# LN1's shift in per-sequence biases, h's low part on VectorE, both normal forms on GpSimd

## The reference, cut to what matters

```python
mod = (_silu(L0_c) @ L0_wmod).reshape(L0_c.shape[0], 6, 1, -1)
sa, ca, ga, sb, cb, gb = (mod[:, 0], mod[:, 1], mod[:, 2], mod[:, 3], mod[:, 4], mod[:, 5])
ga = (2 * (ga >= 0) - 1) * jnp.maximum(jnp.abs(ga), 0.25)      # gb alike
h = _layernorm(x, axis=-1) * (1 + ca) + sa
x = x + ga * attention(h)        # q, k, v = h @ w.T + bias; softmax over |i-j| <= 32; @ wo.T + bo
h = _layernorm(x, axis=-1) * (1 + cb) + sb
x = x + gb * ffn(h)              # top 2 of 8 gated SiLU experts, and the shared one
```

## Time and profile before

| what | value |
|---|---|
| median of 3 runs | 743.09 us (741.37 to 744.73) |
| the profiled execution | 748.45 us |
| its span, first to last instruction | 746.7 us |
| TensorE (PE) busy | 661.9 us, 89% |
| ScalarE (ACT) busy | 590.7 us, 79% |
| VectorE (DVE) busy | 581.9 us, 78% |
| GpSimd (POOL) busy | 567.4 us, 76% |
| DMA, mean over the span | 171 GB/s |
| mean granted TensorE clock | 0.924 |

### The profile page before, as it was taken

How to read it: one execution, slowest core, us unless ns; L and a number is a source line. 1 busy time by engine, 2 the same in 40 slices (tenths; PEclk the granted TensorE clock), 3 DMA queues, 4 the chain that set the end, 5 groups by cost and what they waited for, 6 DMA issues and landing times.

```text
span 746.7 us, 18990 instructions
## 1 busy us (share of the span) xinstructions
PE 661.9 (89%) x5934; PEld 556.9 (75%) x5934; DVE 581.9 (78%) x1541; ACT 590.7 (79%) x2538; POOL 567.4 (76%) x628
## 2 busy tenths in 40 slices
PE   2278898999999999989998999989899989989886
PEld 1167676878878788878887888878788878878775
DVE  5446656988888888979898689888898978867553
ACT  3277777989898989889898689889898988875442
POOL 5440518998989888996988599988979896758784
PEclk9655557999999999999999899999999999999999
DMA  4747675777785867767777668677777676614120
GB/s 146 181 104 181 176 203 138 186 214 191 199 210 170 214 186 202 192 186 205 187 180 192 175 187 206 185 187 209 196 193 207 160 211 158 197 33 137 54 90 14
DMA packets 193860, 127.70 MB, mean 171 GB/s; under 512 B 110640, under 2 KB 170848, under 8 KB 193632
## 3 DMA queue, kind: packets, MB, share of 16 engines
q1 hardware_dynamic: 193760, 126.50, 64.0%
HBM read 96.29 MB, written 30.17 MB: 169 GB/s over the span
## 4 chain that ended last, share of the span: by engine, by line
PE 47%; DMA 17%; SPq 10%; POOL 9%; issue 7%; ACT 6%; DVE 4%; POOLq 0%; DVEq 0%; ACTq 0%
DMA k<-k_scr 11%; PE ps_s L1218 11%; PE ps_Y L1286 10%; SPq L315 6%; PE ps_O L1241 6%; DMA r_scr<-rst 5%; ACT p L686 4%; PE ps_A L1160 3%; POOL xl L503 3%; POOL xs L497 2%; SPq L323 2%; PE ps_A L1162 2%; PE ps_A L1161 2%; PE ps_M L1269 2%; PE ps_B L1160 2%
## 5 line engine op out<-in xcount | busy, mean ns | idle before, releaser
L686 ACT ACTIVATE p<-ps_s,nmx 128x96 f32<-128x96 f32 x1024 | 332.7, 347 | 52.7 <-DVE nmx L886 52.4
L686 ACT ACTIVATION_READ_ACCUMULATOR p<-ps_s,nmx 128x1 f32 x1024 | 218.2, 213 | 0.0
L1218 PE MATMUL ps_s<-k,q 128*128 128x96 f32 x1024 | 168.8, 299 | 54.0 <-DMA k<-k_scr 35.3
L1218 PEld LDWEIGHTS ps_s<-k,q 128*128 128x128 f32 x1024 | 147.6, 211 | 84.5 <-DMA k<-k_scr 42.4
L886 DVE TENSOR_REDUCE nmx<-ps_s 128x4 f32<-128x384 f32 x256 | 137.9, 547 | 59.9 <-PE ps_s L1218 56.2
L503 POOL TENSOR_TENSOR xl<-xs,xh 128x512 fp32r<-128x512 f32 x128 | 162.9, 1278 | 21.1 <-ACT xh L708 21.1
L497 POOL TENSOR_TENSOR xs<-h,sbc 128x512 f32<-128x512 f32 x128 | 163.6, 1284 | 1.8 <-DMA sbc<-s_scr 1.7
L1286 PE MATMUL ps_Y<-w2s,g 128*128 128x128 f32 x1152 | 161.4, 288 | 0.6 <-DVE g L992 0.6
L1286 PEld LDWEIGHTS ps_Y<-w2s,g 128*128 128x128 f32 x1152 | 148.5, 200 | 4.7 <-DVE g L992 0.8
L903 DVE STREAM_TRANSPOSE pt<-p 128x384 f32<-128x384 f32 x256 | 136.6, 558 | 17.3 <-ACT p L686 14.5
L983 DVE SCALAR_TENSOR_TENSOR th<-th,ps_A 128x512 f32<-128x512 f32 x144 | 97.6, 678 | 33.4 <-ACT th L729 32.1
(11 more groups left out here) (119 smaller groups left out, 931.2 us busy)
## 6 DMA issues: line engine op xcount, KB each, us to landing
sbc<-s_scr SPq DMA_DIRECT2D x64, 512.0 KB, 5.6
k<-k_scr SPq DMA_DIRECT2D x64, 384.0 KB
q<-q_scr SPq DMA_DIRECT2D x128, 96.0 KB
k<-k_scr SPq DMA_DIRECT2D x32, 336.0 KB
q_scr<-qh SPq DMA_DIRECT2D x32, 256.0 KB, 2.8
k_scr<-kh SPq DMA_DIRECT2D x32, 256.0 KB, 3.0
xt<-x SPq DMA_DIRECT2D x16, 256.0 KB, 6.1
q_scr<-ql SPq DMA_DIRECT2D x16, 256.0 KB, 2.9
```

The source lines that it names most:

```text
L686: last = nc.scalar.activation(p[:, n % PRING, gg, :], ps_s[:, n % 2, MK * gg:MK * gg + MK], ACT.Exp, bias=nmx[:, n, gg:gg + 1], accum_out= ...
L1218: last = mm(ps_s[:, n % 2, MK * gg:MK * gg + MK], heads[:, h, gg, nl], k4[:, h, gg, :, MB * nl:MB * nl + MB], start=gg == 0, stop=gg == HG ...
```

## The change

- LN1's shift sa is no longer added to h. The projections see h = xn x (1 + ca), and W sa + bias is made once for each sequence at the start, in `bqk` for q and k and `bvs` for v: three matmuls of 16 columns, three VectorE operations, a fourth slice in wqkv (wv in its own order). The matmul through wo now takes `bvs`, one bias for each sequence.
- `modulate` of LN1 and the tile h1 go. `high_h1` makes hh from the PSUM bank M1, with the scale.
- `low_h1` moves from GpSimd to VectorE: hl = scale x M1 - hh from PSUM. Its call stands behind `moments(b-1, l2)` and ahead of `low_q(b+1)`.
- `normal` of LN2 moves from ScalarE (behind `probabilities(b, 8)`) to GpSimd (behind `shift(b-1, l2)`, ahead of `expand_v(b, 0)`).
- SyncE: `put_q`, `put_k`, `load_half`, `spread_scores` and `spread_sums` are cut into smaller calls, called in the same order of DMAs, with further waits (shown). `load_bias` waits for `add_bias` of the sequence before.

```diff
@@ SyncE @@
             def load_bias(b):
+                if b > 0:
+                    sp.wait_ge(xb_d, b)
                 sp.dma_start(brow[:], b_scr[bass.ds(b, 1)].to_broadcast([128, D])).then_inc(b_in, 16)
...
+            def put_ql(b, par):
+
                 sp.wait_ge(q_l, b + 1)
+                if b >= 2:
+                    sp.wait_ge(half_in[0], 112 * (b - 1))
+                    sp.wait_ge(half_in[1], 112 * (b - 1))
                 sp.dma_start(q_scr[par, :, 1].rearrange("j r s -> r j s"), ql[:].bitcast(F32)).then_inc(q_scr_w, 16)
...
+            def put_scores(b):
 
                 sp.wait_ge(smt_cp, b + 1)
+                if b > 0:
+                    for k in range(NE // 2):
+                        sp.wait_ge(s_in[k], 16 * b)
                 sp.dma_start(s_scr, smT[:]).then_inc(s_wr, 16)
...
+            def put_sums(b):
 
                 sp.wait_ge(rst_cp, b + 1)
+                if b > 0:
+                    sp.wait_ge(r_in, 16 * b)
@@ GpSimd @@
-            def low_h1(b):
-
-                pool.wait_ge(l1["hh"], b + 1)
-                nc.gpsimd.tensor_tensor(hl[:], h1[:], hh[:].bitcast(F32), ALU.subtract).then_inc(l1["hl"], 1)
...
                 if has(b, 2):
                     scaled_low(b - 2, 3, par)
-                if has(b, -1, 1):
-                    low_h1(b + 1)
-                if has(b, 2):
                     scaled(b - 2, 4, par)
                 if has(b, 1):
                     spread_var(b - 1, l2, ln2)
                     inverse(b - 1, l2, ln2)
                     shift(b - 1, l2, ln2)
+                    normal(b - 1, l2, ln2, x2[:, 1 - par])
                 if has(b, 0, 1):
                     expand_v(b, 0)
@@ ScalarE @@
-            def normal(b, s, ln, src):
...
             def high_h1(b):
 
-                act.wait_ge(l1["h"], b + 1)
-                if not seq_is(b, 0):
+                act.wait_ge(l1["tr"], b + 1)
+                if b == 0:
+                    act.wait_ge(s_md, 1)
+                else:
                     act.wait_ge(v_mm, b)
                     act.wait_ge(q_mm, b)
-                nc.scalar.activation(hh[:], h1[:], ACT.Copy).then_inc(l1["hh"], 1)
+                nc.scalar.activation(hh[:], ps["M1"][:], ACT.Copy, scale=col(mod, 1, b)).then_inc(l1["hh"], 1)
...
-                nc.scalar.activation(qh[:], ps["M1"][:], ACT.Identity, bias=bqs[:]).then_inc(q_h, 1)
+                nc.scalar.activation(qh[:], ps["M1"][:], ACT.Identity, bias=col(bqk, 0, b)).then_inc(q_h, 1)
...
                 if has(b, -1, 1):
-                    modulate(b + 1, l1, h1[:], 0, "M1")
                     high_h1(b + 1)
...
                 if has(b, 0):
                     probabilities(b, 8, par)
-                if has(b, 1):
-                    normal(b - 1, l2, ln2, x2[:, 1 - par])
-                if has(b, 0):
                     probabilities(b, 9, par)
@@ VectorE @@
+            def low_h1(b):
+
+                dve.wait_ge(l1["hh"], b + 1)
+                nc.vector.scalar_tensor_tensor(hl[:], ps["M1"][:], col(mod, 1, b), hh[:].bitcast(F32),
+                                               ALU.mult, ALU.subtract).then_inc(l1["hl"], 1)
...
+            dve.wait_ge(s_sa, 1)
+            nc.vector.tensor_scalar(bqk[:, 0], ps["M0"][:, 0:B], bia[:, 0:1], SCALE, ALU.add, ALU.mult)
+            nc.vector.tensor_scalar(bqk[:, 1], ps["M0"][:, B:2 * B], bia[:, 1:2], None, ALU.add)
+            nc.vector.tensor_scalar(bvs[:], ps["M0"][:, 2 * B:3 * B], bia[:, 2:3], None, ALU.add).then_inc(s_bq, 1)
             dve.wait_ge(s_bo, 1)
...
             nc.vector.tensor_tensor(mrow[:, 2], mrow[:, 0], bo2, ALU.mult).then_inc(s_mr, 1)
+            low_h1(0)
             low_q(0)
...
                     statistics(b - 1, l2, ln2, x2[:, 1 - par])
                     moments(b - 1, l2, ln2)
                 if has(b, -1, 1):
+                    low_h1(b + 1)
                     low_q(b + 1)
@@ TensorE @@
-            mm(ps["Y"][0:B, 2 * D:3 * D], bia[:, 2:3].to_broadcast([128, B]), wom[:], start=True, stop=True)\
-                .then_inc(s_bo, 1)
+            pe.wait_ge(s_md, 1)
+            for i, k in enumerate((0, 1, 3)):
+                last = mm(ps["M0"][:, i * B:i * B + B], wqf[:, k, :], mod[:, 0, :], start=True, stop=True)
+            last.then_inc(s_sa, 1)
+            pe.wait_ge(s_bq, 1)
+            mm(ps["Y"][0:B, 2 * D:3 * D], bvs[:], wom[:], start=True, stop=True).then_inc(s_bo, 1)
```

More of the change, by code:

```diff
@@ L299, in put_k, with put_kl, load_q @@
                 sp.wait_ge(k_h, b + 1)
[L300 to L301 removed]
+                if b >= 2:
+                    sp.wait_ge(half_in[0], 112 * (b - 1))
+                    sp.wait_ge(half_in[1], 112 * (b - 1))
+                for role in (0, 1):
+                    sp.dma_start(k_scr[par, :, role].rearrange("j r s -> r j s"),
+                                 kh[:].bitcast(F32)).then_inc(k_scr_w, 16)
+            def put_kl(b, par):
                 sp.wait_ge(k_l, b + 1)
+                if b >= 2:
+                    sp.wait_ge(half_in[0], 112 * (b - 1))
+                    sp.wait_ge(half_in[1], 112 * (b - 1))
                 sp.dma_start(k_scr[par, :, 2].rearrange("j r s -> r j s"), kl[:].bitcast(F32)).then_inc(k_scr_w, 16)
[L305 to L312 removed]
+            def load_q(b, h, par):
+                if b > 0:
+                    sp.wait_ge(sc_mm, NMB * b - HB if h == 0 else NMB * b)
                 sp.wait_ge(q_scr_w, 48 * b + 48)
@@ L317, in load_half, with load_k @@
                                  [:, :, HB * h:HB * h + HB]).then_inc(half_in[h], 16)
+            def load_k(b, h, par):
+                keys = k_scr[par].rearrange("j c (d g) s -> (j c d) g s", g=HG)
+                if b > 0:
+                    sp.wait_ge(sc_mm, NMB * b - HB if h == 0 else NMB * b)
                 sp.wait_ge(k_scr_w, 48 * b + 48)
@@ L462, in add_bias, with normal @@
                                         ALU.add).then_inc(xb_d, 1)
-            def low_h1(b):
-                pool.wait_ge(l1["hh"], b + 1)
-                nc.gpsimd.tensor_tensor(hl[:], h1[:], hh[:].bitcast(F32), ALU.subtract).then_inc(l1["hl"], 1)
+            def normal(b, s, ln, src):
+                pool.wait_ge(s["nm"], b + 1)
+                if b > 0:
+                    pool.wait_ge(s["tr"], b)
+                for a in range(NQB):
+                    nc.gpsimd.tensor_scalar(ln["xn"][:, a], src[:, a], ln["rstd"][:, a:a + 1], ln["nm"][:, a:a + 1],
+                                            ALU.mult, ALU.add).then_inc(s["xn"], 1)
             def expand_v(b, h):
@@ L633, in _ @@
             nc.scalar.activation(wqh[:, 1:3], wqf[:, 1:3], ACT.Copy).then_inc(s_wh, 1)
-            def normal(b, s, ln, src):
-                act.wait_ge(s["nm"], b + 1)
-                if not seq_is(b, 0):
-                    act.wait_ge(s["tr"], b)
-                for a in range(NQB):
-                    nc.scalar.activation(ln["xn"][:, a], src[:, a], ACT.Identity, bias=ln["nm"][:, a:a + 1],
-                                         scale=ln["rstd"][:, a:a + 1]).then_inc(s["xn"], 1)
             def modulate(b, s, h, k, bank):
@@ L648, in modulate @@
                     act.wait_ge(s_md, 1)
-                elif s is l1:
-                    act.wait_ge(s["hl"], b)
-                if s is l2 and not (seq_is(b, 0) or seq_is(b, 1)):
+                if b > 1:
                     act.wait_ge(xs_d, NE * (b - 1))
@@ L677, in high_k @@
                     act.wait_ge(k_scr_w, 48 * b)
[L678 removed]
+                nc.scalar.activation(kh[:], ps["M0"][:], ACT.Identity, bias=col(bqk, 1, b)).then_inc(k_h, 1)
             def probabilities(b, n, par):
@@ L729, in expert @@
                 nc.scalar.activation(th[:, par], ps["A"][:], ACT.Tanh, scale=0.5).then_inc(th_d, 1)
-            modulate(0, l1, h1[:], 0, "M1")
             high_h1(0)
@@ L1428 @@
         "w2": np.concatenate([a["L0_ffn_w2"], a["L0_ffn_w2s"]]).transpose(1, 0, 2),
-        "wqkv": np.stack([a["L0_attn_wq"][order], a["L0_attn_wk"][order], a["L0_attn_wv"][vorder]]).transpose(2, 0, 1),
+        "wqkv": np.stack([a["L0_attn_wq"][order], a["L0_attn_wk"][order], a["L0_attn_wv"][vorder],
+                         a["L0_attn_wv"]]).transpose(2, 0, 1),
         "wo": a["L0_attn_wo"].T,
```

64 lines of the change are left out of this document (38 added, 26 removed).

## The result

The changed kernel takes 754.56 us (median of 4 runs, 751.27 to 757.18), the kernel before, run beside it, 742.23 us (740.35 to 744.73): a ratio of 1.0162, 95% interval 1.0108 to 1.0215. Run once more, later, it took 755.66 us, ratio 1.0177 (1.0141 to 1.0212). The profiled execution took 753.45 us.

The account below looks back on a forecast made before the run. TensorE's own instruction stream was taken to bound a full step. Waits of +13.1 us less 2.6 at the start gave +10.5; 743.09 + 10.5 = 753.6, plus 1.5, made 755.0 us, own range 749 to 761, overall 745 to 767.

Parts of the forecast that it names:

- The wait for hl: TensorE ahead of the projections in each full step, hl queued behind VectorE's moments: 1.95 us (1.85 to 2.1).
- The price of hl: `low_h1` on VectorE, priced as the ql row at 0.75 us; bounds 0.69 and 0.75.
- The late keys: Waits at `scores(b, 8)` hide the new wait: full steps cost 7.8 plus 3.6 us, five steps 0.
- its rival: TensorE's clock falls in half of 13 full steps, 1.6 us each: +10 us, 765 us; chance 0.15.
- A loss at each: TensorE's clock falls in each of 13 new waits, 1.6 us each: estimate +21 us, 776 us; no separate chance.
- Start: TensorE's waits for hl(0) and hl(1) shorten by 1.3 us each: -2.6 us (0 to -3).
- Step 1: TensorE at clock 0.5 waits 3.4 us for hl, 1.7 of it within late loads: +1.7 us.
- 0 while covered: GpSimd's added LN2 `normal` calls delay `values(b, 0)`: 0 behind the new wait, 0.8 us a step without it.
- ScalarE's relief: ScalarE loses `modulate` (0.78 us) and four `normal` calls (1.70 us); full steps gain 0, down to -9 us.
- The sum: Whole kernel: 13.1 us of new waits less 2.6 at the start, +10.5 us.
- 1.5 for the median: Added to 753.6 us because an execution with fewer late loads also hides less of the new wait.

## Why the prediction held, point by point

The forecast was 755.0 us. The median is 754.6, and the mechanism is the one named. That the number fits to half a microsecond is luck, as the last point shows. The terms came out so:

- **The wait for hl: 1.95 us forecast.** The trace shows 1.80 as idle time ahead of the projections, 1.96 as the longer way from `attn_out` to them, and 40.65 against 38.60 us, so 2.05, if the undisturbed step is set against that of the kernel before with the keys on time. The price of hl is 0.72 us, between the 0.69 and 0.75 of the earlier trace rows. By the Trainium skill (VectorE: DVE Perf Modes, the section on the TRN2 errata) the estimate was 0.66; the trace has 0.06 more. That it is the queue and nothing else is shown by moving the one call: the wait goes.
- **The late keys: partly mis-sized.** I had the five longest of the earlier trace rows shortened by 1.95 us, with up to 1.1 us of each left. None is left. Part of it is that the longest did not come up: the latest key loads of a full step stand in SyncE's queue 11.19 us behind the start of the step before the change (step 9, from 392.12) and 10.13 us behind it in the changed kernel (step 11, from 479.10):

```profile
403.31 1.92 SPq L323 DMA_DIRECT2D k<-k_scr  x3
```

```profile
489.23 2.06 SPq L345 DMA_DIRECT2D k<-k_scr  x3
```

  The five keys that were 2 us late or more had gone at 10.5 to 11.2, and in this execution of the changed kernel none of a full step went so late. The other part is the cover: in its second execution two loads went at 10.75 and 10.96 us, steps 13 and 11, and TensorE waited for neither. And late keys come back (2.50 and 2.08 us) when the wait for hl is taken away.
- **The clock: the forecast and its rival were both partly true.** What failed is that the two cases stood side by side as exclusive, and that the forecast held before's clock costs fixed. They go with the execution: steps 7, 9 and 14, which cost before 43.01, 45.07 and 42.44 us, took 40.67, 40.65 and 40.66; instead steps 4 and 11 had 1.6 us each. Over four profiled executions with the wait of 1.8 us (the changed kernel twice, with the normal form on ScalarE, with the q gathers moved) the clock fell in 2, 3, 3 and 2 of 13 full steps, for 3.1, 8.7, 5.0 and 6.4 us by the excess over an undisturbed step (in the last, 0.84 us of it is a wait for `scale_o`). That is 5.8 us on average, near the 6.5 of the earlier trace rows. But those 6.5 are of one execution, 6.2 us above its median, so it is not shown that the clock cancels between the medians. The Trainium skill (TensorE: Matmul & The Clock Gate, the section on why this matters) warns of idle gaps between bursts. The runs agree in kind: in the two kernels with no such wait no full step is over 39.8 us; with 1.80 us two or three of 13 are long, with 2.26 us seven. The length of a wait does not decide alone: in step 2 every kernel waits 3.1 us for ScalarE's `probabilities`, and in those two that step is 38.7 and 39.4 us long. The Trainium skill does not say there that each gap costs. A loss at each, by which this kernel would have taken 776 us, is not borne out.
- **Start: -2.6 us forecast, -2.5 measured**, but not in the two equal parts of my working. The wait for hl(0) fell from 2.97 to 1.66 us as forecast. That for hl(1) did not fall from 1.59 to 0.3: it is 1.77. At the first scores the gain already was 37.89 less 35.54 = 2.35 us, so the first part passed on more than its 1.3, and the second gave nothing.
- **Step 1: a wait of 3.4 us, +1.7, forecast; 3.14 us, +1.6, measured.**
- **GpSimd: 0 while covered.** Right, by the run with the normal form on ScalarE. What it costs uncovered was forecast at 0.8 us and is up to 1.90. With hl early, VectorE makes it ahead of the residual, so that the moments come 0.7 us later, and GpSimd's 1.74 come on top. My 0.8 had the second part alone; both make 1.5, and 0.4 of the 1.90 stays unexplained.
- **ScalarE's relief: 0.** Right. It is 31 us less busy, and its wait ahead of `scores(b, 5)` stayed (0.68 in the earlier trace rows, 0.76 in the changed kernel).
- **The sum.** +10.5 us from the profiled pair's terms and 1.5 for the median. The medians are 12.3 apart (interval 8.0 to 16.0 from the ratio), the pair 5.0. For the pair I had put nothing on steps 7, 9, 11, 12 and 14, and they came out at -2.3, -4.4, +1.2, -0.4 and -1.8, together 7.8 us less. The lower clock of step 4 gave 1.3 of it back (42.23 against my 40.9). So for the pair the sum was twice what was measured.
- **Why the medians fit all the same.** The two kernels with the q gathers moved have no late keys in full steps, and tell the price of the change without them: 756.97 - 724.93 = 32.0 us. My terms give 13 x 1.95 + 1.7 - 2.6 = 24.5 for that, with the clock at nothing. Against it stands what late keys and the clock behind them cost in before and no longer in the changed kernel: 741.43 - 724.93 = 16.5, and 1.3 by the other pair (756.97 against 755.66, within the noise), together 17.8 where I had 24.5 - 12 = 12.5. So by this account cost and relief were both put too low, by 7.5 and 5.3 us, and the errors nearly cancelled. It goes by medians, and what of the 16.5 us is keys and what is clock is not shown.

What stays open: why SyncE could issue the keys sooner in the changed kernel's first execution than in the one of before (there is one of before only), and what decides in which execution and step the clock falls.

## What to carry to other kernels

Moving an instruction to an engine with room is not free because the engine has room: ask what stands ahead of it in that engine's queue, and when that can start at the earliest. Here hl's input was ready at 369.2 us, and it was made at 372.7, behind work bound to a matmul of the same step; one call moved up takes the wait away. But covers hide one another: with hl early, the normal form on GpSimd cost up to 1.90 us a step, and with that mended the keys were late. All three mended gave 723.8 us, and the cheapest of them, four gathers put into a time in which their queue only waited, gave nearly all of it (724.9 us) without the change.

## What I had not expected of the hardware

- In the profiled executions a wait of 1.80 us costs only its length in most steps, and one of 2.26 us costs 3.2 us more in seven of 13. Half a microsecond more of waiting in each step gave 25 us.
- The issue of a gather on SyncE depends on what went before it in the queue. Four gathers of 96 KB took 3.35 us behind the load of the sums, 4.25 behind their write, and 7.3 us directly behind the broadcast of the scores (medians of 13 full steps each; the ranges are 3.2 to 4.4, 3.2 to 6.1 and 6.5 to 7.8). Moved within the kernel before, these four were worth -16.5 us at one place of the list (724.93 against 741.43) and +5.4 at another (750.35 against 744.93).
- The granted clock of the record doesn't always tell at which rate matmuls ran. At the start the changed kernel's record says 1.00 where before's says 0.50, while their rows are equally long: the first matmul of the second projection 0.80 us here and 0.79 in the earlier trace rows, against 0.51 in the middle of the run, and from its start to that of the next such row it is 1.44 and 1.45 us. So the mean granted clocks of the two pages (0.987 and 0.924) do not stand for a difference in speed, and I took what the clock costs from the lengths of steps.
